# Cross-attention and a coupled feed-forward block: queries normalised three batches ahead, and a new order of work inside an attention slot

## The chip, the cores and the metric

The kernel runs on one core of a Trainium2 chip. The core has a matrix engine (TensorE, PE in the profile; PEld is its weight load), VectorE (DVE), ScalarE (ACT), GpSimd (POOL) and SyncE (SP), which here issues all transfers. The metric is the device time of one execution in microseconds (us); lower is better. The median of three runs of the kernel before is 1154.41 us (1152.72 to 1155.09).

## What is computed

64 batches of 256 tokens with 256 features attend to 120 context rows each, with 16 heads of 16 features; the softmax is over a clipped (tanh) score with a mask. After a residual and a second normalisation, a small network gives one coupling factor per token, and the features are mixed three times with their "twist", scaled by that factor:

```python
x = x + W_out(softmax(where(mask, -inf, tanh(q k * scale / 4) * exp(log_C))) @ v)   # q = layernorm(x), k = v = ctx
f = layernorm(x); out = f
for _ in range(3):
    tf = sigmoid(net4(gelu(net3(gelu(net2(gelu(net1(out))))))))     # one number per token
    out = out + (0.1 + adaptive_range * (0.7*gf + 0.3*tf - 0.5) * 2) * twist(out)   # gf: one number per batch
x = x + out
```

## The kernel before, in words

**Slots.** Each engine runs its own instruction stream, and all of them walk through the same list of slots (`slots()`, L281). Attention slot i runs from -2 to 66. In slot i the engines work on several batches at once: scores and tanh/exp of batch i, weighted values and division of batch i-1 (`here`), projection, residual and second statistics of batch i-2 (`old`), second normalisation and feature transposition of batch i-3 (LAG = 3), and queries and keys of batch i+1 (`nxt`). When the eighth batch of a group (GROUP = 8) has its features, one "ffn" stage for that group stands between two attention slots. There are eight groups. In this document a slot's place is its position in the group, place = (i - 3) mod 8: the ffn stage comes after place 7, and place 0 is the first slot after it (`after_ffn`, L301).

**ScalarE** in a slot: tanh of the first half of the heads (L835), exp of the second half of the batch before (L841), tanh of the second half, exp of the first half, then the copy of two feature halves of batch i-3 (`features`, L851). In place 7 the last exp follows the features, and the ffn stage starts.

**TensorE** in a slot: first half of the scores (L1067), first weighted values (L1083), query transposes (`queries`, L1042), second half of the scores, key transposes (`keys`, L1051), projection half 0 (`project`, L1098), second weighted values, projection half 1, and the transposes of the normalised features (`norm_to_features`, L1111). `keys` waits for VectorE's copy of the queries (L623), because both use the same PSUM bank; `norm_to_features` waits for VectorE's copy of the keys (L628) for the same reason.

**VectorE** in a slot: `attn_out` half 0 (L637), `attn_features` of batch i-2 (L657), `queries_out` (L623), `keys_out` (L628), first statistics of batch i+2 (`stats`, L612 and L617), `attn_out` half 1, `residual` of i-2 (L662), `divide` of i-1 (L645, L649), `stats_2` of i-2 (L669, L675), `combine` of one batch of the group before (L740, L741), and at places 3 and 5 (HIGH_AT) `high_half` (L684), which splits off the upper half of the features.

**GpSimd** in a slot: `norm_2` of batch i-3 (L419, L420, L422, then twice L428), `factors` for one batch of the group before (twice L483, `twisted`; twice L489, the x part), `values` (L412), `query_hat` of batch i+2 (L394, L395, L397, then twice L403), and at places 3 to 6 (LOW_AT) one `low_half` (L498), which needs `high_half`. At place 0 there is no `query_hat` but the thirteen small operations of `coefficients` (L447); its batch is normalised at the start of the ffn stage instead. The combine of a batch needs the x part, and its store (L334) needs the combine.

**SyncE** in a slot: the store of one batch of the group before, then the loads of batch i+4 (L325 and L330). A load waits for the store of the batch that had its buffer 16 batches before. In the ffn stage it copies the coupling rows (L347).

**Buffers.** The normalised query (`q_hat`) and its statistics have two buffers (b % 2), so `query_hat(b)` waits for the transposes of batch b-2:

```python
if b >= 2:
    eng.wait_ge(s_qtr, b - 1)
eng.wait_ge(s_rstd, b + 1)
```

## Time and profile before

| | |
|---|---|
| median of 3 runs | 1154.41 us |
| the profiled execution's own time | 1158.11 us |
| its span, first to last instruction | 1156.2 us |
| TensorE busy, mean granted clock | 998.3 us (86%), 0.964 |
| ScalarE busy | 928.4 us (80%) |
| VectorE busy | 793.2 us (69%) |
| GpSimd busy | 584.0 us (51%) |
| share of the 16 DMA engines' time taken by the largest queue | 13.0% |

A share is a mean over stages of different kinds: attention slots, in which all five engines work, and ffn stages, in which GpSimd is nearly idle. What an engine does in one kind of stage says nothing of the other, so stretches are read one by one. TensorE's busy time includes waits inside its pipeline; its clock is 1.00 at full speed (2.4 GHz) and 0.5 at half.

### The profile page before, as it was taken

How to read it: one execution, taken by the hardware profiler on the slowest of the kernel's cores; microseconds unless marked ns; L12 is line 12 of the kernel's file. 1: busy time of each engine (PE TensorE's matmuls, PEld its weight loads, DVE VectorE, ACT ScalarE, POOL GpSimd, SP SyncE). 2: the span in 40 equal slices, each digit the busy share in tenths (PEclk: the TensorE clock that was granted, in tenths of full speed). 3: DMA queues.
4: the chain of work that ended last, by engine and by line, in shares of the span. 5: the costliest groups of instructions: out<-in, count | busy, mean ns of one | idle time of the engine just before them, and what ended most of it. 6: DMA issues, size and time to landing. Idle time of an engine off the chain costs nothing.

```text
span 1156.2 us, 21972 instructions
## 1 busy us (share of the span) xinstructions
PE 998.3 (86%) x7260; PEld 536.9 (46%) x7260; DVE 793.2 (69%) x1738; ACT 928.4 (80%) x1153; POOL 584.0 (51%) x1117
## 2 busy tenths in 40 slices
PE   6889988899888998889888898888988889886894
PEld 4555435544455434554355543555435544453431
DVE  4876677757687485874858749577577757676285
ACT  5999679887798777987779877898679887794576
POOL 4577107871188602895048830688207871175303
PEclk8999999999999998999999999999999999997897
DMA  4110002210022100211002200122001220010002
GB/s 129 45 42 19 1 2 68 65 50 1 1 69 69 46 1 2 89 48 46 1 24 69 69 23 2 45 70 69 0 1 47 69 68 1 1 42 28 19 1 74
DMA packets 67281, 43.85 MB, mean 38 GB/s; under 512 B 42081, under 2 KB 50785, under 8 KB 67169
## 3 DMA queue, kind: packets, MB, share of 16 engines
q1 hardware_dynamic: 67168, 42.45, 13.0%
q8 instruction: 60, 0.98, 0.4%
q14 instruction: 53, 0.43, 0.1%
HBM read 25.51 MB, written 16.78 MB: 37 GB/s over the span
## 4 chain that ended last, share of the span: by engine, by line
PE 41%; DVE 21%; issue 14%; ACT 12%; POOL 10%; SPq 1%; DVEq 0%; DMA 0%; POOLq 0%; ACTq 0%
PE ps L1098 7%; PE ps L1143 7%; PE ps L1130 7%; PE ps L1156 5%; ACT probs L835 5%; PE ps L1067 4%; DVE move_u L727 4%; PE ps L1083 3%; ACT probs L841 3%; DVE coup L693 2%; DVE f_t L731 2%; PE ps L1186 2%; DVE move_u L706 2%; DVE move_v L708 2%; PE ps L1165 2%
## 5 line engine op out<-in xcount | busy, mean ns | idle before, releaser
L835 ACT ACTIVATE probs<-ps,u_scale 120x2048 f32<-120x2048 f32 x128 | 253.4, 1980 | 41.5 <-PE ps L1067 40.7
L841 ACT ACTIVATE probs<-probs,exp_bias,clip 120x2048 f32<-120x2048 f32 x128 | 269.5, 2106 | 0.1
L1156 PE MATMUL ps<-h,w 128*128 128x512 f32 x384 | 184.2, 605 | 14.0 <-ACT h L867 13.2
L1067 PE MATMUL ps<-q_t,k_t 32*120 32x256 f32 x2048 | 154.0, 416 | 32.0 <-ACT probs L835 31.2
L447 POOL TENSOR_TENSOR c<-tok_c 128x16 f32<-128x16 f32 x8 | 1.8, 222 | 330.7 <-issue 330.7
L637 DVE STREAM_TRANSPOSE o_t<-ps 128x512 f32<-128x512 f32 x128 | 91.2, 712 | 99.7 <-PE ps L1083 99.6
L1098 PE MATMUL ps<-wo_t,of_t 128*128 128x256 f32 x512 | 149.1, 417 | 8.5 <-DVE of_t L657 8.5
L1083 PE MATMUL ps<-probs,va 120*32 120x256 f32 x2048 | 140.2, 392 | 4.7 <-ACT probs L841 4.7
L1067 PEld LDWEIGHTS ps<-q_t,k_t 32*120 32x120 f32 x2048 | 96.1, 184 | 61.7 <-issue 56.3
L1098 PEld LDWEIGHTS ps<-wo_t,of_t 128*128 128x128 f32 x512 | 94.1, 204 | 44.6 <-issue 26.4
L498 POOL TENSOR_TENSOR f_hl<-f_t,f_hl 128x512 f16<-128x512 f32 x64 | 73.7, 1162 | 79.9 <-DVE f_hl L684 79.9
L1156 PEld LDWEIGHTS ps<-h,w 128*128 128x128 f32 x384 | 66.8, 188 | 89.4 <-issue 64.4
L897 ACT ACTIVATE h<-ps,b 128x512 f32<-128x512 f32 x96 | 65.5, 683 | 43.2 <-PE ps L1156 43.2
L867 ACT ACTIVATE h<-f_t,b 128x512 f32<-128x512 f32 x128 | 85.1, 715 | 13.6 <-DVE f_t L731 9.4
L403 POOL TENSOR_SCALAR q_hat<-xy,neg,rstd 128x256 f32<-128x256 f32 x128 | 86.4, 681 | 11.4 <-POOL rstd L397 11.2
L1130 PE MATMUL ps<-f_hl,w1t_hl 128*128 128x512 f16 x384 | 90.7, 387 | 0.0
L1143 PE MATMUL ps<-f_hl,w_hl 128*128 128x512 f16 x384 | 88.2, 379 | 0.0
L1083 PEld LDWEIGHTS ps<-probs,va 120*32 120x32 f32 x2048 | 54.2, 111 | 71.5 <-issue 38.0
L693 DVE TENSOR_SCALAR coup<-coup,c_tok,c_batch 128x256 f32<-128x256 f32 x128 | 49.0, 425 | 54.9 <-ACT coup L921 53.8
L628 DVE TENSOR_TENSOR k_t<-ps,parity 128x480 f32<-128x480 f32 x64 | 42.1, 658 | 58.0 <-PE ps L1051 58.0
L428 POOL TENSOR_SCALAR f_hat<-xy,neg,rstd 128x256 f32<-128x256 f32 x128 | 70.5, 559 | 13.3 <-POOL rstd L422 13.3
L684 DVE CAST f_hl<-f_t 128x1024 f16<-128x1024 f32 x32 | 22.3, 697 | 77.2 <-PE ps L1143 77.2
(129 smaller groups left out, 1849.6 us busy)
## 6 DMA issues: line engine op xcount, KB each, us to landing
xy<-in_x_dram SPq DMA_DIRECT2D x64, 256.0 KB, 2.9
out_dram<-xy SPq DMA_DIRECT2D x64, 256.0 KB, 2.0
cbuf<-in_ctx_dram SPq DMA_DIRECT2D x64, 120.0 KB, 2.7
tok_c<-coup SPq DMA_DIRECT2D x256, 0.5 KB, 2.0
move_v<-in_L_xattn_W_out_dram SPq DMA_DIRECT2D x1, 256.0 KB, 5.3
move_u<-in_L_ffn_cn_w_dram SPq DMA_DIRECT2D x1, 256.0 KB, 5.6
w<-in_L_ffn_cn_w_dram SPq DMA_DIRECT2D x1, 128.0 KB, 5.5
g<-in_L_ffn_gc_w_dram SPq DMA_DIRECT2D x1, 128.0 KB, 4.0
```

The lines of the kernel that those rows point to most:

```text
L403: eng.tensor_scalar(q_hat[:, b % 2, t, :], xy[:, b % XR, t * E:(t + 1) * E], neg1[:, b % 2, t:t + 1], rstd1[:, b % 2, t:t + 1], ALU.add, A ...
L498: eng.tensor_tensor(f_hl[:, slot, 1, k], f_t[:, k, tok], f_hl[:, slot, 0, k], ALU.subtract) \
L637: eng.transpose(o_t[:, b % 2, 2 * n:2 * n + 2].rearrange("p c q r -> p (c q r)"), banks(PV_BANKS[n])).then_inc(s_ot, 1)
L835: eng.activation(probs[:, b % 2, n * HALF:(n + 1) * HALF, :].rearrange("k h q -> k (h q)"), banks(SCORE_BANK, 4)[0:KEYS, :], ACT.Tanh, sca ...
L841: eng.activation(p, p, ACT.Exp, scale=clip[0:KEYS, 0:1], bias=exp_bias[:, b:b + 1]).then_inc(s_exp, 1)
L867: eng.activation(h1[:, p % 2, m, :], source, ACT.Gelu, bias=b1[:, m:m + 1], scale=by) \
L1067: last = eng.matmul(banks(SCORE_BANK + r)[0:KEYS, odd * S:(odd + 1) * S], k_t[rows, b % 2, odd, n, :], q_t[rows, b % 2, n, :], start=True, ...
L1083: last = eng.matmul(banks(PV_BANKS[n])[j * SLOT:(j + 1) * SLOT, (c % 2) * S:(c % 2 + 1) * S], va[:, b % 3, h, :], probs[:, b % 2, h, :], s ...
L1098: last = eng.matmul(banks(X_BANK)[:, t * E:(t + 1) * E], of_t[:, k, t * P:(t + 1) * P], wo_t[:, k, :], start=(k == 0), stop=(k == EK - 1))
L1130: last = eng.matmul(banks(V_BANKS[m]), w1t_hl[:, w, k, m * P:(m + 1) * P], halves[:, f, k, :], start=(n == 0), stop=(n == len(PRODUCTS) - 1))
L1143: last = eng.matmul(banks(U_BANKS[m]), w1_hl[:, w, k, m * P:(m + 1) * P], halves[:, f, k, :], start=(n == 0), stop=(n == len(PRODUCTS) - 1))
L1156: last = eng.matmul(banks(bank), w2[:, k, :], h1[:, p % 2, k, :], start=(k == 0), stop=(k == EK - 1))
```

## The change

**Rings.** `q_hat`, `mv1`, `rstd1`, `var1` and `neg1` have four buffers (QR = 4), and the waits follow.

**When queries are normalised.** Up to slot 10, as before, batch i+2. Then: three batches in the ffn stage (for places 2, 3, 4), none at places 0, 1 and 4, batch i+3 at places 2 and 3, batch i+2 at places 5, 6 and 7. The first statistics on VectorE move with them.

**GpSimd's order.** `query_hat` and `norm_2` are split into a scale part (the small operations) and the normalisation proper, and `factors` into `twisted_part` and `x_part`. A slot is now: twisted, scale of `norm_2`, x part, `norm_2`, scale of the query, values, `query_hat`, `low_half`.

**TensorE's order.** Projection half 0 stands before the key transposes.

**VectorE's order.** `attn_out` half 0, `queries_out`, `stats`, `combine`, `high_half` (now at places 2 and 4), `keys_out`, `attn_out` half 1, `divide`, `attn_features` (now of batch i-1, one slot earlier than before), `residual`, `stats_2`. At place 0 the combine stays last.

**SyncE's order.** The loads stand before the store; the third batch of the ffn stage is loaded there, ahead of the coupling rows, and place 0 loads nothing.

```diff
-        HIGH_AT = (3, 5)
+        HIGH_AT = (2, 4)
+        def ahead_in_slot(i):
+            if i < GROUP + LAG:
+                return i + 2 if i >= 0 else None
+            at = (i - LAG) % GROUP
+            return None if at in (0, 1, 4) else i + 3 if at < 4 else i + 2
+        def ahead_in_ffn(g):
+            early = g * GROUP + GROUP + LAG
+            return [b for b in range(early + 2, early + 5) if b < NB]
...
                 if kind != "attention":
+                    for b in ahead_in_ffn(i)[2:]:
+                        load(b)
                     coupling_rows(i)
                     late = list(range(i * GROUP, (i + 1) * GROUP))
                     continue
-                for b in late[:1]:
-                    store(b)
-                late = late[1:]
...
-                elif 0 <= i + 4 < NB and i >= -1:
+                elif 0 <= i + 4 < NB and i >= -1 and not after_ffn(i):
                     load(i + 4)
+                for b in late[:1]:
+                    store(b)
+                late = late[1:]
...
             def query_hat(b):
-                if b >= 2:
-                    eng.wait_ge(s_qtr, b - 1)
+                at = b % QR
+                if b >= QR:
+                    eng.wait_ge(s_qtr, b - QR + 1)
...
                 if kind == "ffn":
+                    ahead = ahead_in_ffn(i)
+                    for b in ahead[:2]:
+                        query_scale(b)
+                        query_hat(b)
+                    for k in range(EK):
+                        low_half(i, 2, k)
+                    for b in ahead[2:]:
+                        query_scale(b)
+                        query_hat(b)
+                    for k in range(EK):
+                        low_half(i, 3, k)
...
+                if after_ffn(i):
+                    if i - LAG < NB:
+                        norm_2_scale(i - LAG)
+                        norm_2(i - LAG)
+                    coefficients(groups_before(i) - 1)
+                for b in late[:1]:
+                    twisted_part(b)
+                if 0 <= i - LAG < NB and not after_ffn(i):
+                    norm_2_scale(i - LAG)
+                for b in late[:1]:
+                    x_part(b)
+                late = late[1:]
+                if 0 <= i - LAG < NB and not after_ffn(i):
                     norm_2(i - LAG)
+                if new is not None and 2 <= new < NB:
+                    query_scale(new)
                 if 0 <= i + 1 < NB:
                     values(i + 1)
+                if new is not None and 2 <= new < NB:
+                    query_hat(new)
...
# VectorE
                     if 0 <= here < NB:
                         attn_out(here, 0)
-                    if 0 <= old < NB:
-                        attn_features(old)
                     if 0 <= nxt < NB:
                         queries_out(nxt)
+                    if new is not None and 2 <= new < NB:
+                        stats(new)
+                    if not after_ffn(i):
+                        for b in late[:1]:
+                            combine(b)
+                    if i >= LAG and (i - LAG) % GROUP in HIGH_AT:
+                        high_half((i - LAG) // GROUP, HIGH_AT.index((i - LAG) % GROUP))
+                    if 0 <= nxt < NB:
                         keys_out(nxt)
-                    if 2 <= new < NB and i != early:
-                        stats(new)
                     if 0 <= here < NB:
                         attn_out(here, 1)
+                        divide(here)
+                        attn_features(here)
                     if 0 <= old < NB:
                         residual(old)
-                    if 0 <= here < NB:
-                        divide(here)
-                    if 0 <= old < NB:
                         stats_2(old)
-                    for b in late[:1]:
-                        combine(b)
+                    if after_ffn(i):
+                        for b in late[:1]:
+                            combine(b)
...
# TensorE
                     if 0 <= i < NB:
                         scores(i, 1)
+                    if 0 <= old < NB:
+                        project(old, 0)
                     if 0 <= nxt < NB:
                         keys(nxt)
-                    if 0 <= old < NB:
-                        project(old, 0)
```

## Rows read from the trace of the kernel before

**Rows 1.** Groups of instructions, ScalarE: busy us, mean ns, idle before and its releaser.

```profile
L835 ACT ACTIVATE probs<-ps,u_scale 120x2048 f32<-120x2048 f32 x128 | 253.4, 1980 | 41.5 <-PE ps L1067 40.7
```

**Rows 2.** Windows of single slots, places 1 and 5: length, busy of each engine, clock, DMA.

```profile
320.24:328.62 8.38, 7.36 (x86) 4.62 (x81) 6.40 (x15) 8.38 (x10) 7.76 (x15) 1.00 0.25 79
...
354.90:365.83 10.93, 9.09 (x86) 5.44 (x85) 7.34 (x19) 8.74 (x8) 9.89 (x20) 0.84 0.19 61
```

**Rows 3.** The chain that ended last, places 4 and 5: start us, us, what.

```profile
356.37 1.26 POOL q_hat L403 x2
357.68 0.66 PE ps L1042 x4
```

**Rows 4.** Timeline, places 4 to 5: start us, us, engine, line, idle before in brackets.

```profile
357.68 0.66 PE L1042 MATMUL ps<-ident,q_hat 128*128 128x128 f32 x4 [1.84 <-POOL q_hat L403]
...
359.91 1.97 ACT L835 ACTIVATE probs<-ps,u_scale 120x2048 f32<-120x2048 f32 x1 [1.06 <-PE ps L1067]
```

**Rows 5.** Timeline, GpSimd in place 4: one whole turn of its list.

```profile
348.14 1.16 POOL L498 TENSOR_TENSOR f_hl<-f_t,f_hl 128x512 f16<-128x512 f32 x1 [1.29 <-DVE f_hl L684]
349.39 0.24 POOL L419 TENSOR_SCALAR var<-mv 128x2 f32<-128x2 f32 x1
...
350.81 1.10 POOL L428 TENSOR_SCALAR f_hat<-xy,neg,rstd 128x256 f32<-128x256 f32 x2 [0.21 <-POOL rstd L422]
351.89 1.10 POOL L483 TENSOR_SCALAR twisted<-xy,neg,b_r 128x256 f32<-128x256 f32 x2
352.96 1.10 POOL L489 TENSOR_SCALAR xy<-xy,x_fac,x_add 128x256 f32<-128x256 f32 x2
...
354.98 0.23 POOL L394 TENSOR_SCALAR var<-mv 128x2 f32<-128x2 f32 x1
...
358.84 0.24 POOL L419 TENSOR_SCALAR var<-mv 128x2 f32<-128x2 f32 x1
```

**Rows 6.** Windows from place 1 to place 7, six groups: one, and the sum of six.

```profile
320.24:375.07 54.83, 46.69 (x492) 28.88 (x487) 43.73 (x106) 51.33 (x50) 47.85 (x88) 0.97 0.23 72
...
sum 330.30, PE 280.65 PEld 174.00 DVE 263.82 ACT 308.21 POOL 288.30; mean PE 46.77 PEld 29.00 DVE 43.97 ACT 51.37 POOL 48.05
```

**Rows 7.** Windows from place 7 to the next place 0: six groups' sum, and the first group.

```profile
sum 447.74, PE 410.33 PEld 192.14 DVE 287.13 ACT 335.06 POOL 128.08; mean PE 68.39 PEld 32.02 DVE 47.85 ACT 55.84 POOL 21.35
...
98.37:171.41 73.04, 67.33 (x338) 31.50 (x334) 46.70 (x92) 55.81 (x89) 17.23 (x32) 1.00 0.03 1
```

**Rows 8.** Timeline, VectorE in places 3 to 5.

```profile
347.37 0.68 DVE L684 CAST f_hl<-f_t 128x1024 f16<-128x1024 f32 x1
...
353.36 0.69 DVE L662 TENSOR_TENSOR xy<-xy,ps 128x512 f32<-128x512 f32 x1 [0.31 <-PE ps L1098]
353.97 0.35 DVE L645 RECIPROCAL inv_sum<-o_t 128x32 f32<-128x32 f32 x1
...
355.91 0.41 DVE L740 TENSOR_TENSOR xy<-xy,twisted 128x256 f32<-128x256 f32 x1
...
356.56 0.71 DVE L637 STREAM_TRANSPOSE o_t<-ps 128x512 f32<-128x512 f32 x1
```

**Rows 9.** Timeline, TensorE in place 1: the feature transposes.

```profile
326.61 0.60 PE L1111 MATMUL ps<-ident,f_hat 128*128 128x128 f32 x4
```

**Rows 10.** Single lines: duration ns min/median/max, first and last start.

```profile
L403 POOL TENSOR_SCALAR q_hat<-xy,neg,rstd x128: 549/558/1138, 7.0 to 1033.3; 128x256 f32<-128x256 f32 x128
...
L428 POOL TENSOR_SCALAR f_hat<-xy,neg,rstd x128: 554/557/584, 42.7 to 1072.6; 128x256 f32<-128x256 f32 x128
...
L741 DVE TENSOR_TENSOR xy<-xy,twisted x56: 410/418/1378, 180.8 to 1075.7; 128x256 f32<-128x256 f32 x56
```

**Rows 11.** Timeline, ScalarE at the start of the tail: the last exp.

```profile
1049.73 2.10 ACT L841 ACTIVATE probs<-probs,exp_bias,clip 120x2048 f32<-120x2048 f32 x1
```

**Rows 12.** Window of the tail, from the last batch's first tanh to its features.

```profile
1041.33:1074.34 33.01, 18.23 (x121) 11.25 (x117) 18.45 (x41) 12.18 (x18) 21.32 (x39) 0.76 0.09 33
```

**Rows 13.** Waits, longest first: engine line, releaser: us in total, times, longest.

```profile
POOL c L447 <- issue: 330.7, 8, 44.4
```

82 lines of the change are left out of this document (38 added, 44 removed).

## The prediction

> **What bounds the kernel now.** First the groups of instructions. All idle time of ScalarE before its tanh is 41.5 us, 40.7 of it put down to the scores [rows 1]. Then single slots. A slot at place 1 takes 8.38 us and ScalarE is busy for all of it [rows 2]: 8.38 us is what a slot costs when ScalarE alone decides. Place 5 takes 10.93 us with ScalarE busy for 8.74 and GpSimd for 9.89, and TensorE's granted clock falls from 1.00 to 0.84 [rows 2]. The chain that ended last says why: there it runs along GpSimd to `query_hat` and goes over to the query transposes [rows 3]. TensorE stood idle 1.84 us before these transposes, the second half of the scores came late, and tanh waited 1.06 us [rows 4]. The reader should see a queue: queries are not slow, they stand at the end of GpSimd's list.
>
> GpSimd's list has a length that can be read off [rows 5]. From 349.39 to 358.84, without waits of note, it takes 9.45 us: scale and `norm_2` 2.50 (349.39 to 351.89), twisted and x part with values 3.09 (to 354.98), query and `low_half` 3.86. `low_half` alone is 1.25 (348.14 to 349.39), so the query is 2.61. In front of the first `low_half` stands a wait of 1.29 for `high_half`, which VectorE does at the end of the slot [rows 5]. Over places 1 to 7 the list is 7 x 8.20 + 4 x 1.25 = 62.4 us, against 7 x 8.38 = 58.7 of ScalarE. GpSimd loses about half a microsecond per slot, and from place 4 on nothing is left to hide it.
>
> What is lost: from place 1 to place 7 (six slots) the six groups after an ffn stage take 330.30 us [rows 6]; at 8.38 per slot they would take 301.7. So 28.6 us. From place 7 to the next place 0 they take 447.74 us [rows 7]; the first group, which has no factors on GpSimd, takes 73.04, and six times that is 438.2. So 9.5 us more. Together 38.1 us can be had there.
>
> **The change, part by part.**
> *Queries ahead.* Two of the eight queries leave the slots for the ffn stage. GpSimd's list over places 1 to 7 becomes 7 x 5.59 + 5 x 2.61 + 4 x 1.25 = 57.2 us, under ScalarE's 58.7. In the ffn stages GpSimd waits 330.7 us in 8 waits, up to 44.4 each [rows 13], which hides the two moved queries (5.2 us) and their statistics; without that cover they would cost 5.2 per group. Cost 0. The transposes now find their query ready except near place 7: the batch needed at place 7 is made at place 6, only one slot before.
>
> *`high_half` a slot earlier.* The 1.29 wait at two places goes [rows 5]. It is part of the 28.6.
>
> *Projection before keys.* TensorE does 1 us of projection while VectorE copies the queries. VectorE's `attn_features` a slot earlier makes it possible. No own gain in the sum, since ScalarE decides.
>
> *The new serial loop.* `keys_out` now stands behind `combine`, this behind the x part, this behind the scale of `norm_2`, this behind `stats_2`, the last work of VectorE's slot. Once round: scale 1.42 (349.39 to 350.81), x part 1.06 [rows 5]; combine 0.65 (355.91 to 356.56), `keys_out`, `attn_out`, `attn_features` and `residual` at about 0.65 each (the residual's 353.36 to 353.97 is 0.61), divide and `stats_2` 1.94 (353.97 to 355.91) [rows 8]; sum 7.7 us, with `high_half` (0.68) 8.4. That is at or under 8.38, so by itself it costs nothing, but it has no reserve at places 2 and 4.
>
> *`norm_2` later in the list.* Counted from tanh, `stats_2` ends at about 1.2 us of the next slot. Then scale 1.42, x part 1.06, `f_hat` 1.1: 4.8. The feature transposes start now at 326.61, 6.4 us into their slot [rows 9], and can start at about 6.7 before the next scores are late. At places 3, 5 and 6 the list is 9.45, 1.07 over ScalarE. Followed through (place 4: 2.2, place 5: 2.2 through the loop, place 6: 3.3, place 7: about 4.1 as the start of the scale), `f_hat` ends 0.2 late at place 6 and 0.5 late at place 7.
>
> *Port.* In the old order the combine overlaps `query_hat`, whose halves take up to 1.138 us against a usual 0.558, while `f_hat`, which has no combine beside it, never exceeds 0.584 [rows 10]. In the new order the combine starts with `f_hat`. Bounds: 0, or 0.58 per half; taken 0.3 in all, since the median of L403 is the undisturbed one. So the lateness is 0.5 per group at place 6 and 0.75 at place 7. The Trainium skill (SBUF — State Buffer, Who interferes with whom) states that a VectorE instruction with two SBUF inputs contends with a GpSimd instruction that reads SBUF, and that the second one to issue blocks. The trace agrees for L403; if it held `f_hat` for both combine halves each time, each group would lose 0.5 us more and the gain would be 33.6 us.
>
> *SyncE.* Load before store, and a third load ahead of the coupling rows, which wait for factors made much later. The load waits for the previous slot's store. Cost 0; the late stores have only the end of the next slots to meet.
>
> *Start.* Projection before keys may save up to 1 us in slots 1 to 3; splitting the weights stands in between. Bounds -1 and +1, taken 0.
>
> *Tail.* From the last batch's first tanh to its features: 33.01 us at a mean clock of 0.76 [rows 12]. Its last exp ends at 1051.83, 10.5 in [rows 11]. New: weighted values 1.1, `attn_out` 0.7, divide 1.1, `attn_features` 0.65, residual of the batch before 0.65, its `stats_2` 0.9: 15.6. GpSimd: scale 1.42 and x part 1.06 (18.1), `f_hat` 1.1, `low_half` 1.25, twisted 1.07 (21.5), then scale, x part and `f_hat` of the last batch 3.6 and the transposes 0.6: 25.7. Taken 27, as the clock stays low here: 6 us less. Bounds 3 and 8.
>
> Sum: 28.6 - 6 x 0.5 = 25.6; 9.5 - 6 x 0.75 = 5.0; tail 6; together 36.6 us. Against the profiled execution's own 1158.11 us this gives 1121.5; that execution is 3.7 us above the median of the runs, 1154.41, so the predicted median is 1118.
>
> **The rivals.**
> *A. The lateness does not end.* The query needed at place 7 is made at place 6, where the list is 9.45 us and starts 3.3 late; by my count it is ready 2 us into place 7, when it should be ready at 1. If one slot per group keeps a stall like that of place 5 (10.93 - 8.38 = 2.55 [rows 2], the dip of the clock included), 6 x 2.55 = 15.3 come back: 1133. For it: the small slack, 1.5 us per group. Against: in the old order the query of place 5 came 2.7 us into it (357.63 after 354.90 [rows 2, 3]).
>
> *B. Everything hides.* `f_hat` is in time, no clock dip is left, the tail gives 8 and the start 1: 38.1 + 9 = 47: 1107. For it: at place 1 ScalarE is busy all the time already [rows 2].
>
> *C. Slower: the new loop.* If each combine half, released together with `f_hat`, waits as in L741's longest case, 1.378 against 0.418 [rows 10], the loop is 7.7 + 1.9 = 9.6 us, and 10.3 with `high_half`. Six slots then take 59.1 us where they took 55.05 (330.30 / 6): 6 x 4.0 = 24, less the tail's 6: slower by 18, 1172. It decides once the loop passes 9.2 us. Against: L741's median is 0.418 with GpSimd reading SBUF beside it in most slots. The skill's same section says that issue order decides who blocks, and here `f_hat` is issued first; by that rule the combine waits for one half, 0.56, and the loop is 8.3 to 9.0, which no run here shows yet.
>
> *D. A new wait takes the place.* The loop is 8.9 to 9.2 on average and only the tail's gain is left or less: within 0.2% of 1154, or a few us under it.
>
> **How the numbers follow.** About 0.2% (2.3 us) is what a measurement of this kernel can tell from no change. Chances: forecast 0.44 (1113 to 1123 as its own range, from the tail's bounds and the port's), A 0.22, B 0.20, D 0.06 (two thirds of it within 0.2%), C 0.08. Faster 0.88, same 0.04, slower 0.08. The range takes in A and B: 1105 to 1136.
>
> **What would show it.** Right: windows from place 1 to 7 near 50.8 us each with ScalarE above 98% busy; no idle time of TensorE before L1042 at places 4 to 6; the `low_half` waits gone; the clock 1.00 at place 5; place 7 to place 0 near 73.8; the tail near 27. Wrong: idle time of tanh with the scores released late by `keys_out` (C, D), seen as a long gap before L628 that ends with L741; or L1042 still waiting for L403 at place 6 or 7 (A); or L851 waiting for L1111 by more than 1 us in these slots. The forecast would also fall if L740 and L741 grow well above 0.42, or if the ffn stages grow beyond 73 us.

## The result, and the profile after

The changed kernel takes 1144.18 us (median of 4 runs, 1143.15 to 1144.97); the kernel before took 1154.75 beside it (1152.72 to 1156.72). The ratio is 0.9908, 95% interval 0.9889 to 0.9927: 10.6 us faster, where 36.6 was forecast and 1105 to 1136 was the range. The sign was right and the size was not.

The busy times and three groups of instructions of the changed kernel, whose span is 1142.4 us; last, the group of the feature copies in the kernel before:

```profile
PE 988.3 (87%) x7260; PEld 533.2 (47%) x7260; DVE 815.8 (71%) x1738; ACT 925.6 (81%) x1153; POOL 627.6 (55%) x1117
...
L882 ACT ACTIVATE probs<-ps,u_scale 120x2048 f32<-120x2048 f32 x128 | 254.4, 1987 | 26.8 <-PE ps L1114 26.7
...
L452 POOL TENSOR_SCALAR f_hat<-xy,neg,rstd 128x256 f32<-128x256 f32 x128 | 105.1, 828 | 3.1 <-POOL rstd L442 3.1
...
L898 ACT ACTIVATE f_t<-ps 128x256 f32<-128x256 f32 x128 | 48.8, 399 | 36.8 <-PE ps L1158 36.8
...
L851 ACT ACTIVATE f_t<-ps 128x256 f32<-128x256 f32 x128 | 48.7, 397 | 32.3 <-PE ps L1111 32.0
```

ScalarE's idle time before its tanh fell from 41.5 us [rows 1] to 26.8. It was to fall close to nothing. Its wait for the feature transposes did not fall at all: 36.8 us, where it was 32.3. And a pass of `f_hat` takes 0.828 us on average, where none took more than 0.584 before [rows 10].

The stretches between first tanhs, in the changed kernel: places 3, 4, 5 and 6 of one group, then the sums of six groups from place 1 to place 7, of six from place 7 to the next place 0, and the tail. The columns are those of [rows 2].

```profile
473.18:481.57 8.39, 7.54 (x90) 4.82 (x86) 7.80 (x19) 8.39 (x10) 7.81 (x15) 1.00 0.20 70
481.57:491.65 10.08, 7.57 (x86) 4.67 (x82) 6.97 (x15) 8.70 (x11) 9.91 (x16) 1.00 0.22 67
491.65:500.33 8.68, 7.75 (x86) 4.76 (x85) 8.05 (x20) 8.52 (x8) 6.98 (x13) 1.00 0.22 74
500.33:510.22 9.89, 7.75 (x86) 4.70 (x86) 7.60 (x19) 8.63 (x8) 9.55 (x17) 1.00 0.21 67
...
sum 324.59, PE 276.22 PEld 172.50 DVE 270.17 ACT 306.33 POOL 279.97; mean PE 46.04 PEld 28.75 DVE 45.03 ACT 51.06 POOL 46.66
...
sum 444.31, PE 405.23 PEld 188.82 DVE 301.54 ACT 334.56 POOL 164.92; mean PE 67.54 PEld 31.47 DVE 50.26 ACT 55.76 POOL 27.49
...
1031.96:1061.77 29.81, 16.58 (x121) 9.98 (x114) 18.11 (x40) 12.25 (x20) 23.85 (x39) 0.76 0.09 35
```

Place 3 is where the forecast wanted all of them: 8.39 us, ScalarE busy throughout. Place 5 is close to it (8.68 instead of 10.93) and its clock stays at 1.00, which is the 2.4 GHz level, where it was 0.84 before [rows 2]. But place 4 now takes 10.08 and place 6 takes 9.89. The sum from place 1 to place 7 fell by 5.7 us (330.30 - 324.59, [rows 6]), from place 7 on by 3.4 (447.74 - 444.31, [rows 7]), and the tail by 3.2 (33.01 - 29.81, [rows 12]). The start lost 0.7. The remaining 2.2 of the 13.8 by which the two profiled spans differ (1156.2 - 1142.4) lies before the first tanh, in the slots at place 0, in the last group and in what follows the last features.

What makes place 4 late stands in the timeline, here of places 3 and 4 of the group before that one, whose first tanhs start at 336.12, 344.51 and 354.57:

```profile
338.22 0.23 POOL L439 TENSOR_SCALAR var<-mv 128x2 f32<-128x2 f32 x1 [0.32 <-DVE mv L718]
...
343.31 0.69 DVE L692 TENSOR_TENSOR o_n<-o_t,inv_sum 128x512 f32<-128x512 f32 x1
...
343.33 1.39 POOL L432 TENSOR_SCALAR va<-cbuf 120x256 f32<-120x256 f32 x1
...
348.09 0.23 POOL L439 TENSOR_SCALAR var<-mv 128x2 f32<-128x2 f32 x1
...
349.31 1.10 POOL L516 TENSOR_SCALAR xy<-xy,x_fac,x_add 128x256 f32<-128x256 f32 x2
...
350.40 2.05 POOL L452 TENSOR_SCALAR f_hat<-xy,neg,rstd 128x256 f32<-128x256 f32 x2
...
350.45 0.43 DVE L783 TENSOR_TENSOR xy<-xy,twisted 128x256 f32<-128x256 f32 x1 [2.94 <-POOL xy L516]
350.79 0.70 DVE L784 TENSOR_TENSOR xy<-xy,twisted 128x256 f32<-128x256 f32 x1
351.42 0.68 DVE L727 CAST f_hl<-f_t 128x1024 f16<-128x1024 f32 x1
352.02 0.65 DVE L671 TENSOR_TENSOR k_t<-ps,parity 128x480 f32<-128x480 f32 x1
...
352.81 0.63 PE L1158 MATMUL ps<-ident,f_hat 128*128 128x128 f32 x4 [1.66 <-DVE k_t L671]
...
353.47 0.38 ACT L898 ACTIVATE f_t<-ps 128x256 f32<-128x256 f32 x1 [1.12 <-PE ps L1158]
```

The reader should see three things. VectorE stood idle for 2.94 us before the combine, because the x part on GpSimd was not there; `high_half` and `keys_out` queue behind the combine, and TensorE's feature transposes queue behind the keys. The GpSimd pair of `f_hat`, 1.10 us before [rows 5], took 2.05 beside the combine and the cast. And the scale of `norm_2` begins 348.09 - 344.51 = 3.58 us into place 4, where the forecast had 2.2. The transposes start 8.3 us into the slot; the forecast had 6.7 as the latest harmless time, so they are 1.6 late, and the slot is 1.7 longer than 8.39.

Each line by itself, in the changed kernel (duration in ns, min/median/max):

```profile
L784 DVE TENSOR_TENSOR xy<-xy,twisted x56: 417/700/703, 183.5 to 1059.4; 128x256 f32<-128x256 f32 x56
...
L452 POOL TENSOR_SCALAR f_hat<-xy,neg,rstd x128: 557/824/1238, 43.8 to 1059.8; 128x256 f32<-128x256 f32 x128
```

In [rows 10] the same two operations had medians of 418 and 557. Here both lengthen: neither simply waits for the other to end.

### The profile page after: what moved, and what is told of

It reads as the page before. It is cut to its first block, busy times and chain, and to the rows that moved or that the text cites. A ratio compares the mean times of both kernels' runs of the same rounds, so it can differ in the third digit from the quotient of the medians.

```text
span 1142.4 us, 21970 instructions
## 1 busy us (share of the span) xinstructions
PE 988.3 (87%) x7260; PEld 533.2 (47%) x7260; DVE 815.8 (71%) x1738; ACT 925.6 (81%) x1153; POOL 627.6 (55%) x1117
## 4 chain that ended last, share of the span: by engine, by line
PE 31%; DVE 23%; POOL 17%; ACT 14%; issue 14%; DVEq 0%; DMA 0%; POOLq 0%; ACTq 0%; SPq 0%
PE ps L1190 7%; PE ps L1177 7%; ACT probs L882 6%; PE ps L1203 5%; DVE move_u L770 4%; ACT probs L888 3%; PE ps L1114 3%; POOL f_hat L452 3%; POOL rstd L442 2%; POOL xy L516 2%; DVE coup L736 2%; DVE f_t L774 2%; PE ps L1233 2%; DVE move_u L749 2%; DVE o_n L692 2%
## 5 line engine op out<-in xcount | busy, mean ns | idle before, releaser
L882 ACT ACTIVATE probs<-ps,u_scale 120x2048 f32<-120x2048 f32 x128 | 254.4, 1987 | 26.8 <-PE ps L1114 26.7
L1203 PE MATMUL ps<-h,w 128*128 128x512 f32 x384 | 184.2, 605 | 14.4 <-ACT h L914 13.6
L1114 PE MATMUL ps<-q_t,k_t 32*120 32x256 f32 x2048 | 150.7, 408 | 42.3 <-ACT probs L882 41.4
L1145 PEld LDWEIGHTS ps<-wo_t,of_t 128*128 128x128 f32 x512 | 88.9, 193 | 58.8 <-issue 47.6
L452 POOL TENSOR_SCALAR f_hat<-xy,neg,rstd 128x256 f32<-128x256 f32 x128 | 105.1, 828 | 3.1 <-POOL rstd L442 3.1
L914 ACT ACTIVATE h<-f_t,b 128x512 f32<-128x512 f32 x128 | 85.1, 715 | 14.1 <-DVE f_t L774 9.8
L898 ACT ACTIVATE f_t<-ps 128x256 f32<-128x256 f32 x128 | 48.8, 399 | 36.8 <-PE ps L1158 36.8
L423 POOL TENSOR_SCALAR q_hat<-xy,neg,rstd 128x256 f32<-128x256 f32 x128 | 76.3, 602 | 3.8 <-POOL rstd L413 3.6
L914 ACT ACTIVATE h<-ps,b,uv_scale 128x512 f32<-128x512 f32 x64 | 48.9, 776 | 31.2 <-PE ps L1190 31.1
```

The lines of the kernel that those rows point to most:

```text
L423: eng.tensor_scalar(q_hat[:, at, t, :], xy[:, b % XR, t * E:(t + 1) * E], neg1[:, at, t:t + 1], rstd1[:, at, t:t + 1], ALU.add, ALU.mult). ...
L452: eng.tensor_scalar(f_hat[:, t, :], xy[:, at, t * E:(t + 1) * E], neg2[:, at, t:t + 1], rstd2[:, at, t:t + 1], ALU.add, ALU.mult).then_inc ...
L882: eng.activation(probs[:, b % 2, n * HALF:(n + 1) * HALF, :].rearrange("k h q -> k (h q)"), banks(SCORE_BANK, 4)[0:KEYS, :], ACT.Tanh, sca ...
L914: eng.activation(h1[:, p % 2, m, :], source, ACT.Gelu, bias=b1[:, m:m + 1], scale=by) \
L1114: last = eng.matmul(banks(SCORE_BANK + r)[0:KEYS, odd * S:(odd + 1) * S], k_t[rows, b % 2, odd, n, :], q_t[rows, b % 2, n, :], start=True, ...
L1145: last = eng.matmul(banks(X_BANK)[:, t * E:(t + 1) * E], of_t[:, k, t * P:(t + 1) * P], wo_t[:, k, :], start=(k == 0), stop=(k == EK - 1))
```

## The experiments

Two theories stood at the start: that the engines' sharing (combine beside `f_hat`) is what takes the gain, and that the new order on VectorE, with keys behind the combine, does. Twelve kernels were run. All are edits of the changed kernel unless it is said otherwise; a ratio is to the kernel before, run on the same chip, whose medians were 1152.53 to 1154.92.

**Keys ahead of the combine.**

```diff
+                    if 0 <= nxt < NB:
+                        keys_out(nxt)
                     if not after_ffn(i):
                         for b in late[:1]:
                             combine(b)
                     if i >= LAG and (i - LAG) % GROUP in HIGH_AT:
                         high_half(...)
-                    if 0 <= nxt < NB:
-                        keys_out(nxt)
```

> The changed kernel with keys_out put ahead of combine and high_half on VectorE, nothing else moved. Reference: the changed kernel takes 10.08 us at place 4, 8.68 at place 5, 9.88 at place 6 and 73.99 from place 7 to place 0, where 8.39, 8.39, 8.39 and 73.04 are ScalarE's own; median 1144.2. Theory 1 (GpSimd's list, lengthened by the port and ordered with norm_2 last, makes f_hat late; the copy of the keys is late by nearly the same): f_hat ends only about 0.15 us before the copy of the keys does, so the feature transposes gain 0.1 to 0.4 us per stall; places 4 and 6 stay above 9.3; median 1138 to 1143; TensorE's wait before L1158 is then put down to GpSimd's f_hat. Rival 2 (the copy of the keys behind combine is the wait): places 4 and 6 fall to 8.4 to 8.7 and the median to 1118 to 1125.

Measured: 1127.54 us, ratio 0.9783 (0.9768 to 0.9797); by the two ratios 14.4 us under the changed kernel. From place 1 to place 7 the six groups take 310.87 us instead of 324.59. One slot of each group is still long, place 4 (window), and what the transposes now wait for is `f_hat` itself (waits: us in total, times, longest):

```profile
474.67:484.31 9.64, 7.59 (x86) 4.67 (x82) 7.16 (x16) 8.70 (x11) 9.47 (x15) 1.00 0.21 67
...
PE ps L1158 <- POOL f_hat L452: 20.6, 15, 5.0
```

The time lies between the two ranges: place 6 fell to 8.39, as rival 2 wanted, and place 4 stayed long behind `f_hat`, as theory 1 had it. The place of the keys was a large part of the loss, but the edit also moved the combine in time: `f_hat` is stretched less often (mean 0.741 us instead of 0.828), so not all of the 14.4 us is the keys'.

**`norm_2` in its old place ahead of the twisted part, keys behind the combine as in the change.**

```diff
+                if 0 <= i - LAG < NB and not after_ffn(i):
+                    norm_2_scale(i - LAG)
+                    norm_2(i - LAG)
                 for b in late[:1]:
                     twisted_part(b)
-                if 0 <= i - LAG < NB and not after_ffn(i):
-                    norm_2_scale(i - LAG)
                 for b in late[:1]:
                     x_part(b)
                 late = late[1:]
-                if 0 <= i - LAG < NB and not after_ffn(i):
-                    norm_2(i - LAG)
```

> The changed kernel with GpSimd's old order inside a slot: scale, norm_2, twisted, x part; VectorE's order stays as changed, so keys_out still waits for combine and this for the x part. Theory 1 together with the twin wait (both f_hat and the copy of the keys must come in time): f_hat is early, but the x part ends about 1.1 us later where GpSimd waits for stats_2, so the copy of the keys is later and the slots get longer: median 1150 to 1170, slower than the changed kernel, the wait before L1158 put down to L671. Rival 3 (f_hat alone is what is late): places 4 and 6 fall below 8.8, median 1118 to 1125.

Measured: 1211.3 us, ratio 1.0513 (1.0483 to 1.0543). The two waits that carry it:

```profile
DVE xy L782 <- POOL xy L516: 140.3, 49, 4.8
...
PE ps L1157 <- DVE k_t L670: 71.4, 42, 3.7
```

The direction was forecast and the size was not. `f_hat` is ready early, hardly stretched (mean 0.608 us), and nothing is won: VectorE waits 140.3 us for the x part (66.2 in the changed kernel), and all that stands behind the combine waits too. This is the serial loop that the forecast priced at 7.7 us, made 2.2 us longer by twisted and `f_hat` ahead of the x part.

**Both edits together** (the two diffs above).

> Both moves: keys_out ahead of combine on VectorE and norm_2 ahead of twisted and x part on GpSimd. Theory 1 with the twin wait: both waits go together, places 4 to 6 come to 8.4 to 8.7 and place 7 to place 0 to 73.1 to 73.5, so 4 us per group or some 25 us: median 1117 to 1125. Rival 4 (GpSimd's list is simply too long, whatever its order): a stall stays at places 5 to 7 of 1 us or more each, now before L1089 (query transposes) or at VectorE's combine with attn_out behind it; median 1130 to 1140.

Measured: 1174.49 us, ratio 1.0195 (1.0178 to 1.0212); neither theory nor rival had it slower than before. The keys are out of it; what stands behind the combine is now `high_half`, `o_t` and the residual, for which the projection waits (23.7 us in all, up to 6.0), and it still loses 22 us against the kernel before:

```profile
DVE xy L782 <- POOL xy L516: 96.7, 49, 4.8
```

So a combine in the middle of VectorE's list is what makes a late x part expensive, whatever the neighbour.

**The combine without its second SBUF input.** Each half is replaced by a reduction of `xy` over 256 columns that waits and signals as before. The twisted part is thereby not added, in all groups but the last, so this kernel leaves out a part of the computation.

```diff
-                eng.tensor_tensor(y[:, :, 0:4:3, :], y[:, :, 0:4:3, :], other[:, :, 2:0:-1, :], ALU.add)...
-                eng.tensor_tensor(y[:, :, 1:3, :], y[:, :, 1:3, :], other[:, :, 3::-3, :], ALU.subtract)...
+                for t in range(TT):
+                    eng.tensor_reduce(scratch[:, 2 * b + t:2 * b + t + 1], xy[:, b % XR, t * E:(t + 1) * E],
+                                      AX.X, ALU.max).then_inc(s_res, 1)
```

> The changed kernel with the two operations of combine (two inputs in SBUF each) replaced by two reductions of the same 256 columns with one input, at the same place in the order; so the twisted part is not added in all groups but the last. If the slowing of f_hat (mean 0.828 us against 0.559 before) comes from sharing with combine, its mean falls to 0.56 to 0.60, and the second half of the combine (0.70) has a counterpart of 0.35 to 0.45; then place 4 falls from 10.08 to 9.0 to 9.4 and place 6 from 9.88 to 9.1 to 9.4, and the time by 6 to 12 us. If it does not come from there, f_hat stays at 0.8 and the slots stay.

Measured: one run, 1114.96 us, 37.6 under the kernel before beside it. The groups of the two partners, place 4, and in the middle of it the cast of `high_half` (L728) beside the values:

```profile
L453 POOL TENSOR_SCALAR f_hat<-xy,neg,rstd 128x256 f32<-128x256 f32 x128 | 76.3, 605 | 3.1 <-POOL rstd L443 3.1
...
L782 DVE TENSOR_REDUCE scratch<-xy 128x1 f32<-128x256 f32 x112 | 41.6, 413 | 49.9 <-POOL xy L517 49.9
...
472.68:481.49 8.81, 7.58 (x86) 4.68 (x82) 6.52 (x15) 8.59 (x11) 8.64 (x14) 1.00 0.19 65
...
478.09 0.92 DVE L728 CAST f_hl<-f_t 128x1024 f16<-128x1024 f32 x1
478.43 1.29 POOL L433 TENSOR_SCALAR va<-cbuf 120x256 f32<-120x256 f32 x1
```

The reduction takes 0.413 us, about what a half of the combine takes undisturbed, at the same place and with the same waits; but it reads one input and writes one column. `f_hat` falls from 105.1 to 76.3 us, and with it the slots: 304.53 from place 1 to place 7 against ScalarE's 301.7, and 438.26 from place 7 on against 438.2. With the sharing of the combine gone the new order does what the forecast said of it (1118). So the order of the change alone does not cost the gain; it needs the stretched passes to do so. Not all sharing is gone, though: the cast starts in the last part of an `f_hat` pass and takes 0.92 us instead of 0.68, and the values, which start under it, take 1.29 instead of 0.87, with no instruction of two SBUF inputs beside them on VectorE. Which of the two differences of the reduction did it, one input fewer or nearly nothing written, this run cannot say.

**The combine at the end of VectorE's slot** (as it stands after an ffn stage in the change), all else of the change kept.

```diff
-                    if not after_ffn(i):
-                        for b in late[:1]:
-                            combine(b)
...
-                    if after_ffn(i):
-                        for b in late[:1]:
-                            combine(b)
+                    for b in late[:1]:
+                        combine(b)
```

> The changed kernel with combine as the last work of VectorE's slot, as in the old order; GpSimd's order stays as changed. Now nothing of the slot stands behind the x part. Theory 5 (the stall is made of two things: the copy of the keys waits for the x part behind combine, and the port makes f_hat, and so the x part of the next slot, late): f_hat no longer starts together with combine, its mean goes to 0.56 to 0.62, places 4 and 6 fall to 8.4 to 8.8 and place 7 to place 0 to 73.0 to 73.4; median 1115 to 1125, better than keys_out first alone (1127.5). Rival 6 (the length of GpSimd's list is the limit): places 4 to 6 keep 0.5 us or more each and the median stays at 1127 to 1133.

Measured: 1117.47 us (5 runs, 1116.97 to 1125.46), ratio 0.9696 (0.9666 to 0.9727): the best kernel of the study, by the ratios 24.5 us under the changed one. The profiled execution is the one of 1125.46. Most of its slots take 8.39 us, but place 4 takes 9.74 to 9.83 in four of the six groups. One of these, and the rows of its end:

```profile
476.78:486.52 9.74, 7.56 (x86) 4.63 (x81) 8.99 (x20) 8.66 (x10) 9.57 (x14) 1.00 0.21 67
...
483.09 1.59 POOL L452 TENSOR_SCALAR f_hat<-xy,neg,rstd 128x256 f32<-128x256 f32 x2
...
483.61 0.72 DVE L692 TENSOR_TENSOR o_n<-o_t,inv_sum 128x512 f32<-128x512 f32 x1
...
484.73 0.66 PE L1154 MATMUL ps<-ident,f_hat 128*128 128x128 f32 x4 [1.34 <-POOL f_hat L452]
```

The time came as expected, the mean of `f_hat` did not: 0.665 us, above the 0.56 to 0.62. `f_hat` has a new neighbour, the divide's `o_n`, also with two inputs in SBUF, and takes 1.59 beside it in this slot. At the end of the slot the combine holds up nothing. As in the run with the keys ahead, part of the 24.5 us is a shorter `f_hat` and not the place of the combine by itself.

**Combine last, and `norm_2` in its old place** (that diff and the one of the second experiment).

> The changed kernel with combine last on VectorE and GpSimd's old order (scale, norm_2, twisted, x part). Norm first was ruinous while combine stood in the middle of VectorE's list (1211, and 1174 with the keys ahead). Theory 5 says that it was so only through combine's wait for the later x part, with attn_out and divide behind it; with combine last it costs nothing: places 4 to 6 at 8.4 to 8.6, median 1113 to 1122. Rival: norm first itself costs, by the x part meeting stats_2 late; then the median is above 1130.

Measured: 1135.83 us, ratio 0.9852 (0.9828 to 0.9877). Place 4 falls to 8.7 to 9.0 us, but place 6 takes 11.4 to 12.8:

```profile
PE ps L1084 <- POOL q_hat L423: 20.0, 10, 2.5
```

The query needed at place 7 is late. That is the forecast's rival A, a mechanism that the changed kernel itself does not show.

**GpSimd: twisted, scale, `norm_2`, x part; VectorE: keys ahead of `high_half`, combine last.**

```diff
                 for b in late[:1]:
                     twisted_part(b)
                 if 0 <= i - LAG < NB and not after_ffn(i):
                     norm_2_scale(i - LAG)
+                    norm_2(i - LAG)
                 for b in late[:1]:
                     x_part(b)
                 late = late[1:]
-                if 0 <= i - LAG < NB and not after_ffn(i):
-                    norm_2(i - LAG)
...
-                    if i >= LAG and (i - LAG) % GROUP in HIGH_AT:
-                        high_half(...)
                     if 0 <= nxt < NB:
                         keys_out(nxt)
+                    if i >= LAG and (i - LAG) % GROUP in HIGH_AT:
+                        high_half(...)
```

> The version that should beat both: the changed kernel with combine last on VectorE (as in the run with 1117.5), keys_out ahead of high_half, and GpSimd's order twisted, scale, norm_2, x part. In the run with combine last the one stall left was f_hat ending 1.2 us late at place 4 in some groups, behind the x part. With the x part behind norm_2, f_hat comes 1.1 us earlier. Theory 5: no slot from place 1 to 7 above 8.5 but for single dips of the clock, 50.3 to 51.0 a group, median 1109 to 1117. Rival (GpSimd's list is now at its limit and the last in it, the query for place 7, gets late, as with norm first: 1135.8): place 6 or 7 at 9.5 or more, waits before the query transposes, median 1120 to 1136.

Measured: 1130.33 us (6 runs, 1125.39 to 1132.92), ratio 0.9808 (0.9781 to 0.9835). Worse than combine last alone, by the same wait as in the kernel just shown: the query transposes wait 18.2 us for `q_hat`, in 12 waits of up to 2.4. Whatever is put ahead of the queries at the places with a list of 9.45 us shows up at place 7. The rival was right: GpSimd's list has no room left.

**The old orders, queries ahead alone.** The kernel before with the rings, loads and times of the queries changed, `HIGH_AT` at (3, 5), and the orders on GpSimd, VectorE and TensorE as before, but for the scale of the query, which stands ahead of the values as in the change. As a diff of the kernel before, shortened:

```diff
+    QR = 4
...
+        def ahead_in_slot(i):
...
+        def ahead_in_ffn(g):
...
-                if 2 <= i + 2 < NB and i != early:
-                    query_hat(i + 2)
+                if new is not None and 2 <= new < NB:
+                    query_hat(new)
```

> One part alone: the kernel before with the rings of four, the queries ahead and the third load in the ffn stage (loads before the store, query scale before values); VectorE's, TensorE's and GpSimd's orders and HIGH_AT as before. If the reading of the kernel before was right (GpSimd's list of 62.4 us over places 1 to 7 against ScalarE's 58.7, now 57.2), most of the 38.1 us of stalls go: places 1 to 7 at 50.4 to 51.5 a group, median 1117 to 1128, so below the whole change's 1144. If the queries were not the limit, it stays above 1140.

Measured: 1142.67 us (10 runs, 1139.30 to 1150.83), ratio 0.9918 (0.9893 to 0.9942): of 38 us, some 10. TensorE's waits for `q_hat` fall from 28.9 us to 13.3, and yet place 4 takes 9.20 us where ScalarE is busy for 8.64. Places 4 and 5, and the group of `low_half`:

```profile
478.87:488.07 9.20, 7.57 (x86) 4.74 (x85) 6.96 (x16) 8.64 (x10) 7.48 (x14) 1.00 0.24 70
488.07:497.03 8.96, 7.56 (x86) 4.72 (x85) 7.34 (x19) 8.62 (x8) 8.41 (x16) 1.00 0.25 75
...
L525 POOL TENSOR_TENSOR f_hl<-f_t,f_hl 128x512 f16<-128x512 f32 x64 | 74.2, 1169 | 44.5 <-DVE f_hl L726 44.5
```

Slot by slot, moving the queries changed one place. Places 3, 4 and 6 took 8.6, 9.2 and 9.2 us before and take 8.5, 9.2 and 9.2 to 9.5 now. Place 5 took 10.93 to 10.99 in five of the six groups, at a granted clock of 0.84, and 9.46 in the one group in which the clock stayed at 1.00 there; now it takes 8.7 to 9.0, always at 1.00. The six stretches from place 1 to 7 sum to 315.6 us instead of 330.3, and some 10 of these 14.7 us go with the clock, which no longer falls in these slots (an estimate: 5 x 1.5 at place 5, by the slot of 9.46, and 2.2 in one slot at place 6).

GpSimd itself waits 44.5 us for `high_half`, where it waited 79.9. The chain that ended last shows who does not wait (start us, us, what; pieces of one turn):

```profile
480.54 0.69 DVE f_hl L726
481.22 0.62 DVE o_t L679
...
482.44 0.59 DVE q_t L665
...
483.16 0.40 PE ps L1095 x2
483.56 0.87 PE ps L1142 x4
484.43 1.00 PE ps L1127 x16
485.43 1.07 PE ps L1142 x4
```

This is a loop between VectorE and TensorE: copy of the queries, then on TensorE keys, projection, weighted values and projection, then on VectorE residual, divide, `stats_2`, combine, `attn_out`, `attn_features` and the next copy of the queries. From one copy of the queries to the next a turn takes 8.6 to 8.7 us, and 9.2 with `high_half` in it; in the kernel before the same copies lie 8.6 and 9.2 us apart at places 2 and 3. So the kernel before had two limits, one behind the other. The same kernel shows why projection goes before keys: TensorE stood idle before the keys, waiting for the copy, with projections at hand:

```profile
483.16 0.40 PE L1095 MATMUL ps<-ident,cbuf 120*128 120x120 f32 x2 [1.04 <-DVE q_t L665]
```

**The same with `HIGH_AT` at (2, 4).**

```diff
-        HIGH_AT = (3, 5)
+        HIGH_AT = (2, 4)
```

> The run with the queries ahead alone (1142.7), with high_half moved to places 2 and 4 and nothing else. There GpSimd waits 44.5 us in all for high_half before low_half, and places 4, 5 and 6 take 9.2, 8.7 to 9.0 and 9.2 to 9.4. If this wait is what kept the queries ahead from paying, it falls to about 15 and the places to 8.4 to 8.7: 2 to 3 us a group, median 1124 to 1131. If the old orders of VectorE and TensorE are the limit (keys behind the copy of the queries, attn_features in the middle), it stays above 1137.

Measured: 1153.13 us (10 runs, 1149.81 to 1159.36), ratio 1.0000 (0.9978 to 1.0022). GpSimd's wait for `high_half` does fall:

```profile
L525 POOL TENSOR_TENSOR f_hl<-f_t,f_hl 128x512 f16<-128x512 f32 x64 | 74.4, 1173 | 14.3 <-DVE f_hl L726 14.3
```

30 us less waiting on GpSimd, and 10 us more time. Moving `high_half` a slot earlier helped nobody in the old order, since GpSimd was no longer what everything waited for. Why it costs 10 us can be read in part from its trace: `low_half`, which now starts at once, runs while VectorE does the combine.

```profile
651.88 1.36 POOL L525 TENSOR_TENSOR f_hl<-f_t,f_hl 128x512 f16<-128x512 f32 x1
...
652.14 1.38 DVE L783 TENSOR_TENSOR xy<-xy,twisted 128x256 f32<-128x256 f32 x1
```

A half of the combine usually takes 0.42 us. Here 14 of the 112 take 1.04 to 1.42, together 10.8 us more; with `HIGH_AT` at (3, 5) one did. VectorE is in the loop that sets the time there, so this is about the size of the loss, but it was not tried by itself.

**The new orders of the change, queries at their old times.**

```diff
         def ahead_in_slot(i):
-            if i < GROUP + LAG:
-                return i + 2 if i >= 0 else None
-            at = (i - LAG) % GROUP
-            return None if at in (0, 1, 4) else i + 3 if at < 4 else i + 2
+            return i + 2 if i >= 0 and not after_ffn(i) else None
         def ahead_in_ffn(g):
-            return [b for b in range(early + 2, early + 5) if b < NB]
+            return [b for b in range(early + 2, early + 3) if b < NB]
...
-                elif 0 <= i + 4 < NB and i >= -1 and not after_ffn(i):
+                elif 0 <= i + 4 < NB and i >= -1:
```

> The other part alone: the changed kernel with the queries at their old times (batch i+2 in each slot but place 0, one in the ffn stage), everything else as changed. Theory: the new orders cost by themselves. GpSimd's list is 62.4 us again, and it is lengthened by the port (f_hat 0.5 us per slot, values 0.5 in some), so about 66 us over places 1 to 7, and the copy of the keys waits behind it: 8 to 14 us per group above the changed kernel less what overlaps; median 1165 to 1200, slower than before. Rival: the new orders are worth something by themselves (projection between, no wait for high_half): median 1140 to 1150.

Measured: 1147.33 us (7 runs), ratio 0.9960 (0.9937 to 0.9982). The rival's range holds: the new orders do not cost by themselves.

**The same, combine last** (with the diff of that experiment).

> The fourth corner of a square: the changed kernel with combine last on VectorE (1117.5) but with the queries at their old times. The other corners: before 1153 to 1155, queries ahead in the old orders 1142.7, both 1117.5. Reading A (two limits lay one behind the other in the kernel before: GpSimd's list of 62.4 us a group, and a loop of VectorE and TensorE through the copy of the queries, the keys, the projection and the residual, 8.6 us a slot and 9.2 with high_half; each hides the gain of lifting the other): the orders alone give little, because GpSimd's list is back at 62.4 us and more, places 4 to 6 at 9.2 to 10.5, median 1138 to 1150, and the two gains alone (10 and at most 15) add up to less than the 36 of both. Reading B (the orders alone do it, queries ahead was needless): median 1115 to 1125.

Measured: 1135.71 us, ratio 0.9837 (0.9822 to 0.9853), just under reading A's range and far from B's. VectorE's and TensorE's loop is no longer what counts (place 4 takes 8.5 us), and GpSimd's list is: place 5 takes 10.19 us, and the query transposes wait 18.6 us for `q_hat`. With these the parts can be laid side by side, as gains over the kernel before ((1 - ratio) x 1154 us):

| | queries at old times | queries ahead |
|---|---|---|
| old orders | 0 | 9.5 |
| new orders, combine in the middle | 4.6 | 10.6 |
| new orders, combine last | 18.8 | 35.1 |

Read down: the orders are worth more than the queries. Read the last row and the first: together they give 7 us more than their sum (35.1 against 28.3), as two limits one behind the other do. The intervals of the three ratios leave this at about 7 plus or minus 5. The first row has `HIGH_AT` at (3, 5) and the others at (2, 4); in the old orders with the queries ahead and (2, 4) the gain is 0, and the difference would be larger. In the middle row together they give less than the sum (10.6 against 14.1). Read the middle row: the combine in the middle of VectorE's list costs 24.5 us with the queries ahead and 14.2 without.

**The kernel before with the reductions for the combine** (the diff of the reductions; the twisted part is not added there either), to see what the combine costs in the old order.

> The kernel before with combine's two operations replaced by two reductions with one input at the same place (end of VectorE's slot); the twisted part is not added but in the last group. In the old order the combine meets query_hat, whose mean is 0.681 us. If the port is a cost there too, the mean falls to 0.60 or less, and since the query is last in GpSimd's list and decides from place 4 on, the time falls by 3 to 12 us; GpSimd's list stays too long by itself, so the stalls of places 4 to 6 stay at 9.0 or more. If the port costs nothing there: within 2 us of the kernel before.

Measured: one run, 1149.2 us. The median of the kernel before beside it is 5.5 above that, but its 17 runs go from 1146.96 to 1157.88, so a single run does not tell this from no change. And the query is not faster for it:

```profile
L404 POOL TENSOR_SCALAR q_hat<-xy,neg,rstd 128x256 f32<-128x256 f32 x128 | 87.6, 691 | 11.4 <-POOL rstd L398 11.2
```

0.691 us without the combine, 0.681 with it. The forecast had put the long queries of the kernel before down to the combine. The timeline of that kernel in place 3 shows another partner, the divide's `o_n`:

```profile
477.63 0.69 DVE L649 TENSOR_TENSOR o_n<-o_t,inv_sum 128x512 f32<-128x512 f32 x1
...
477.74 1.55 POOL L403 TENSOR_SCALAR q_hat<-xy,neg,rstd 128x256 f32<-128x256 f32 x2 [0.17 <-POOL rstd L397]
```

## Why the prediction was wrong in size

In short: the step that failed is *Port*, taken at 0.3 us in all. Passes of VectorE and GpSimd that run beside each other are 0.3 to 1 us longer, in nearly every slot, and they stand in a list and a loop without reserve. With the combine's share of this taken away the time was 1114.96 us, some 27 us lower, which is the gain that is missing. The same lengthening hurts much less where nothing queues behind the combine (1117.47 us).

**What bounds the kernel: half right.** GpSimd's list was one limit. That the 38.1 us between it and ScalarE's 8.38 us could be had by shortening the list was wrong: the old orders with the queries ahead get 9.5 of them, nearly all in the slot at place 5. The forecast looked at one chain, in the slot with the longest stall [rows 3], and took what lay under it to be ScalarE at once. The loop of VectorE and TensorE lay between, at 8.6 and 9.2 us per turn. Had it been added up from the durations, it would have been seen: [rows 8] have its VectorE part.

**Queries ahead, cost 0: right.** No run shows a wait in the ffn stages for it. In the changed kernel TensorE waits 9.6 us in all for `q_hat`, 0.8 at most.

**`high_half` a slot earlier: its term was no term.** The 1.29 us wait at two places is a wait of GpSimd and was worth nothing once GpSimd did not set the time. Done behind the queries in the old orders it costs 10 us; in the new orders it was not tried by itself.

**Projection before keys, no own gain: open.** The new orders, of which it is one, give 4.6 us with the queries left where they were, and 18.8 with the combine last. TensorE's wait for the copy of the queries before the keys (20.6 us in 30 waits before) is gone in the changed kernel. How much of the gain is the projection's and how much is `attn_features`' or the divide's was not taken apart.

**The new serial loop, 7.7 and 8.4, "by itself it costs nothing": nearly right by itself, wrong as it ran.** In the run with the reductions a turn with `high_half` takes 8.7 us, and place 4 is 0.4 longer than ScalarE needs. In the changed kernel the scale of `norm_2` starts 329.24 at place 2 and 338.22 at place 3: 8.98 us with `high_half` in it. The second half of the combine is 0.28 longer here, and `o_n` takes 0.88 instead of 0.69. From place 3 to place 4 it is 9.87, without a wait, and this is GpSimd's list, forecast as 9.45. The working: `f_hat` beside the combine 1.53 instead of 1.10, the values beside `o_n` 1.39 instead of 0.87, the query 1.09 instead of 1.25 and the two waits of 0.21 and 0.17 for `rstd` [rows 5] gone; 9.45 + 0.43 + 0.52 - 0.16 - 0.38 = 9.86. The starts drift from 1.51 us into place 2 to 2.10 and 3.58, where 2.2 was forecast for place 4. The loop had no reserve, as the forecast said, and the stretched passes went on top of it.

**`norm_2` later in the list: the rule was right, the lateness was mis-sized and in another place.** Its rule that transposes later than 6.7 us delay the slot one for one holds at place 4. Its own figures do not give the 0.5 at place 7: a start of 4.1 and 3.6 us of scale, x part and `f_hat` make 7.7, which is 1.0 late, so another 3 us over six groups were missing from the sum before anything ran. Forecast was a lateness of 0 at place 4, 0.5 at place 6 and 0.75 at place 7, port included. Place 4 lost 10.08 - 8.39 = 1.69, place 5 0.3, place 6 1.5, and from place 7 to place 0 0.95 (73.99 - 73.04), 4.4 us in a usual group instead of 1.25. The sums over six groups leave 22.9 + 6.1 = 29.0 us over ScalarE's time, where 3.0 + 4.5 were forecast: 21.5 of the 26 us that are missing.

**Port: the step that failed.** 0.3 us in all was taken, from the median of L403, and it was put in once, behind `f_hat` at places 6 and 7. The sharing acts in nearly every slot and in three places: in `f_hat` itself, in the length of GpSimd's list and in the loop through the combine. The bound of 0.58 for one half of `f_hat` held on the average of a pair. Measured, a pair of `f_hat` takes 0.43 more beside the combine and 0.95 more beside combine and cast, L784 takes 0.28 more, and the values 0.52 more. The reason for the low value was drawn from the wrong partner: in the kernel before, halves of `q_hat` take 0.96 to 1.06 us beside `o_n` and 1.06 to 1.14 beside the cast of `high_half`, the longest (507.00) among these, but 0.70 to 0.79 at most with only the combine and what follows it beside them. The run with reductions in the combine's place says what the sharing costs when all that queues behind it is counted: some 27 us, from a single run (37.6 under the kernel before beside it, against the change's 10.6). In the old order it is 5.5 or nothing. The place of the combine is the other half of the cause: with it last, and the sharing less but not gone, 24.5 us come back.

The Trainium skill (SBUF — State Buffer, Who interferes with whom) says that a VectorE instruction with two SBUF inputs contends with a GpSimd instruction that reads SBUF. The trace agrees: two-input combine, `f_hat` 0.828; one-input reduction, 0.605. It also says that the second one to issue is blocked. Where `o_n` issues ahead of the query, `o_n` keeps its 0.69 and the query pays, as it says; but beside the combine both lengthen, L784 by 0.28 and the `f_hat` pair by 0.43.

**Rival C** had the place right, keys behind a combine that waits with `f_hat`, and its price too high: it wanted the loop at 9.6, 10.3 with `high_half`, and 6 x 4.0 us. Measured from scale to scale, places 2 to 7 lie 8.98 to 9.88 us apart, and the 9.87 to 9.88 among these is GpSimd's list. The 1.378 that it took for a half of the combine is one beside `low_half` in the kernel before, not beside a normalisation. It shows in full only where the x part is made later still (1211.3 us). **Rival A** did not occur in the changed kernel; it does in the two kernels that put more ahead of the queries.

**Tail: 3.2 instead of 6, at the lower bound of 3.** The timeline of the changed kernel's tail, VectorE and TensorE:

```profile
1052.97 0.42 DVE L783 TENSOR_TENSOR xy<-xy,twisted 128x256 f32<-128x256 f32 x1 [2.44 <-POOL xy L516]
...
1053.93 0.68 DVE L705 TENSOR_TENSOR xy<-xy,ps 128x512 f32<-128x512 f32 x1
```

The last residual waits behind a combine that waits for the x part, the same queue as at place 4; the working had added VectorE's items up without that wait. **Start:** 0.7 us worse, inside its bounds.

**SyncE: 0.** The only wait for a load of `x` is 0.6 us, once, in both kernels, so nothing speaks against it; it was not tried by itself.

## What to carry to other kernels

When one limit is to be removed, add up the next one before pricing the gain: every closed loop through two engines' queues, from the same durations, not only the engine that the profile's longest wait names. A step that waits for another engine belongs at the end of its queue, and behind it nothing that a third engine needs: the same combine costs 24.5 us more in the middle of VectorE's list than at its end, where it also shares less with `f_hat`. Where an edit puts two-input VectorE work beside a GpSimd pass, price both at their stretched durations, and with what queues behind them.

## What was not expected of the hardware

- A GpSimd pass over 128x256 pairs has levels: 1.10 us alone, 1.53 beside the two halves of the combine, 2.05 with a cast of 128x1024 right behind them. The cast has one input only, and yet it lengthens GpSimd's passes: the run with the reductions shows it beside the values (1.29 instead of 0.87), where no combine is near.
- In the changed kernel L784 takes 0.68 to 0.70 us in 49 of 56 times and its partner L783 0.43 beside the same `f_hat`: the first half is not slowed and the second is. The other seven times, 0.42 us each, are at place 0, where the combine comes last.
- A half of the combine usually takes 0.42 us, but 1.04 to 1.42 beside `low_half` (14 times with `HIGH_AT` moved in the old orders).
- The stretching follows the place in time, not the instruction. With the combine last, `f_hat` meets `o_n` instead and takes 1.59; before, `q_hat` did and took 1.55; in the change, the values do and take 1.39.
- Runs of one kernel spread by very different amounts: 1116.97 to 1125.46 for combine last, 1139.30 to 1150.83 for queries ahead alone, 1146.85 to 1157.81 for 16 runs of the kernel before beside them, but 1143.15 to 1144.97 for the change. The long runs have the lower granted clock: 0.962 at 1157.81 and 0.973 at 1146.85, 0.965 at 1150.83 and 0.978 at 1139.30. What tips them was not found. In the profiled execution of combine last the slot at 450.20 to 460.00 takes 9.80 us at a granted clock of 0.83.
